# Cross-attention scores in three blocks of four key tiles, and all value products of a batch in one place

## What is computed

```python
q = proj(x1, Wq, bq); k = proj(ctx, Wk, bk); v = proj(ctx, Wv, bv)      # 16 heads of 32
scores = clip(einsum('bhsd,bhtd->bhst', q, k) / sqrt(32), -50, 50)
probs = softmax(where(mask, scores, -50))
out = einsum('bhst,bhtd->bhsd', probs, v) @ Wo.T + bo
x2 = layernorm(x1 + layernorm(clip(rs, 0, 0.3) * out))
```

## Time and profile before

| | |
|---|---|
| median of 3 runs | 1448.34 us (1447.04 to 1449.28) |
| profiled execution, its own time | 1448.77 us |
| its span in the trace | 1446.6 us |
| PE busy | 1415.2 us, 98% |
| DVE busy | 1061.0 us, 73% |
| ACT busy | 681.8 us, 47% |
| POOL busy | 534.1 us, 37% |

### The profile page before, as it was taken

The page is one execution under the profiler, slowest core; times in us unless marked ns, Lnnn a source line. Parts: engine busy times, 40 slices in busy tenths (PEclk is TensorE's granted clock), DMA queues, the critical chain, the costliest instruction groups (busy, mean ns, idle before and its releaser), DMA issues. The chain is left out here.

```text
span 1446.6 us, 31910 instructions
## 1 busy us (share of the span) xinstructions
PE 1415.2 (98%) x13340; PEld 1128.1 (78%) x13340; DVE 1061.0 (73%) x2136; ACT 681.8 (47%) x931; POOL 534.1 (37%) x499
## 2 busy tenths in 40 slices
PE   8999999999999999999999999999999997999998
PEld 4889898987888888888888888888888885555343
DVE  5888676554667777777787768778767777677898
ACT  2444444442434334433343443343343334888996
POOL 1000000000344444445445444444444442753576
PEclk9999999999999999999999999999999999999999
DMA  6526433232221121111211211211211221438895
GB/s 225 164 99 176 131 111 121 94 134 91 99 72 51 45 77 51 52 57 51 79 44 51 72 44 43 79 51 45 71 44 54 69 62 39 108 124 323 279 345 205
DMA packets 93886, 149.41 MB, mean 103 GB/s; under 512 B 14002, under 2 KB 61746, under 8 KB 91954
## 3 DMA queue, kind: packets, MB, share of 16 engines
q1 hardware_dynamic: 93746, 147.41, 31.1%
HBM read 101.25 MB, written 44.04 MB: 100 GB/s over the span
## 5 line engine op out<-in xcount | busy, mean ns | idle before, releaser
L912 POOL TENSOR_TENSOR xa_psum<-xa_pr 125x448 f32<-125x448 f32 x126 | 153.0, 1214 | 300.7 <-DVE xa_pr L1135 300.7
L1135 DVE TENSOR_SCALAR xa_pr<-xa_pr,xa_keep 125x448 f32<-125x448 f32 x384 | 152.2, 453 | 131.5 <-ACT xa_pr L964 131.5
L964 ACT ACTIVATE xa_pr<-xa_bSC 125x1344 f32<-125x1344 f32 x128 | 165.6, 1294 | 120.8 <-PE xa_bSC L1259 120.7
L939 ACT ACTIVATE xa_kf<-xa_bKV,xa_bk 128x376 f32<-128x376 f32 x128 | 73.7, 576 | 192.0 <-PE xa_bKV L1178 192.0
L945 ACT COPY xa_v<-xa_bKV 125x512 f32<-125x512 f32 x96 | 56.3, 586 | 206.8 <-PE xa_bKV L1189 201.1
L1178 PE MATMUL xa_bKV<-left_xn,wA 128*128 128x376 f32 x768 | 149.8, 343 | 0.0
L915 POOL TENSOR_TENSOR xa_psum<-xa_psum,xa_pr 125x448 f32<-125x448 f32 x126 | 146.1, 1159 | 9.9
L1178 PE MATMUL xa_bKV<-xa_cx,wA 128*128 128x376 f32 x768 | 149.3, 343 | 0.0
L1189 PE MATMUL xa_bKV<-wZ,left_xn 128*125 128x512 f32 x576 | 142.0, 395 | 2.1 <-POOL xa_ones L881 1.9
L1189 PE MATMUL xa_bKV<-wZ,xa_cx 128*125 128x512 f32 x576 | 141.1, 393 | 0.0
L1178 PEld LDWEIGHTS xa_bKV<-left_xn,wA 128*128 128x128 f32 x768 | 130.0, 188 | 8.9 <-issue 5.3
(11 more groups left out here) (256 smaller groups left out, 2440.2 us busy)
## 6 DMA issues: line engine op xcount, KB each, us to landing
wraw<-in_ctxT SPq DMA_DIRECT2D x32, 752.0 KB, 4.8
ff_hr<-h_scratch SPq DMA_DIRECT2D x28, 512.0 KB, 6.5
wraw<-in_w SPq DMA_DIRECT2D x7, 1024.0 KB, 5.3
xa_qf<-q_scratch SPq DMA_DIRECT2D x32, 224.0 KB, 4.8
xa_x<-x_scratch SPq DMA_DIRECT2D x28, 256.0 KB, 4.9
x_scratch<-xa_x SPq DMA_DIRECT2D x28, 256.0 KB, 2.0
h_scratch<-ff_hq SPq DMA_DIRECT2D x8, 896.0 KB, 5.1
h_scratch<-ff_hs SPq DMA_DIRECT2D x8, 896.0 KB, 5.3
```

The source lines that it names most:

```text
L912: nc.gpsimd.tensor_tensor(psum01[:], third(h, 0), third(h, 1), ALU.add).then_inc(p01_ok, 1)
L964: nc.scalar.activation(pr[h][:], bSC[0:TW, :, 0:TC * S], ACT.Exp, scale=XSCALE).then_inc(exp_ok, 1)
L1135: nc.vector.tensor_scalar(third(h, t), third(h, t), EM50, bound, ALU.max, ALU.min).then_inc(pr_ok, 1)
```

## The change

It does five things at once.

1. The 12 (head group, key tile) pairs of a batch are scored in three blocks of four tiles, in place of four blocks of three. `score_pieces` says which tiles of which group a block holds. The exponential of a block is two ACT instructions, since a block spans two groups.
2. `attend` of all four groups and then `sums` of both pairs of groups stand in one place, behind the first score block of the next batch. Two groups share a bank: values in the columns 0 to 223, sums in 224 to 447.
3. `psum` is one tile of two groups' width in place of two tiles of one group; one `sums` handles a pair with products 224 wide.
4. DVE's `attended` handles a pair: reciprocal and product are 224 wide. Both stand at the start of the next batch's body. `tail2` and `tail3` both stand at the end of the body.
5. POOL's `norm2` moves from ahead of group 3's sums to the end of the body. PE does keys 0, values 0, keys 1, values 1 of the next batch in a row behind the last score block.

The core of the diff:

```diff
-        psum01, psum = n.sb("psum01", [TW, NJ, S]), [n.sb(f"psum{i}", [TW, NJ, S]) for i in range(2)]
+        psum01, psum = n.sb("psum01", [TW, NJ, S]), n.sb("psum", [TW, NJ, 2 * S])
...
+        score_pieces = (((0, 0, 3, 0), (1, 0, 1, 3)), ((1, 1, 2, 0), (2, 0, 2, 2)), ((2, 2, 1, 0), (3, 0, 3, 1)))
...
# POOL
                 for h in range(C):
-                    if h == 3 and tail is not None and not last(b):
-                        norm2(tail)
                     if not (last(b) and h >= 2):
...
-                        wait(pool, sum_done, 4 * b + h - 1)
-                        nc.gpsimd.tensor_tensor(psum[h % 2][:], psum01[:], third(h, 2), ALU.add).then_inc(ps_ok, 1)
+                        if h % 2 == 0:
+                            wait(pool, sum_done, 2 * b + h // 2)
+                        nc.gpsimd.tensor_tensor(psum[:, :, value_columns(h)], psum01[:], third(h, 2), ALU.add).then_inc(ps_ok, 1)
...
+                if tail is not None and not last(b):
+                    norm2(tail)
# DVE
             def body(b, par, pair):
+                if not first(b):
+                    attended(b - 1, 0)
+                    attended(b - 1, 1)
+                limits(b, 0)
+                if not last(b):
+                    split_low(b + 1, 1 - par)
+                limits(b, 1)
...
+                if tail is not None:
+                    tail1(tail)
+                limits(b, 2)
...
+                if tail is not None and not last(b):
+                    tail2(tail)
+                    tail3(tail)
# PE
+            def sums(b, p):
+                pe.wait_ge(ps_ok, 4 * b + 2 * p + 2)
                 for j in range(NJ):
+                    mm = nc.tensor.matmul(bPV[p][j * HD:(j + 1) * HD, 2 * S:4 * S], ones[0:TW, :], psum[:, j, :], start=True, stop=True)
                 mm.then_inc(sum_done, 1)
...
+            def attend_pairs(b, par, pairs):
+                for p in pairs:
+                    attend(b, par, 2 * p)
+                    attend(b, par, 2 * p + 1)
+                for p in pairs:
+                    sums(b, p)
...
+                scores(b, par, 0)
+                if third_value(b):
+                    keys(b, par, 2)
+                if not first(b):
+                    attend_pairs(b - 1, 1 - par, range(2))
+                if third_value(b) == 0:
+                    keys(b, par, 2)
+                    values(b, par, 2)
+                scores(b, par, 1)
+                keys(b, par, 3)
+                if third_value(b):
+                    values(b, par, 2)
+                if tile_of(b - 1) is not None:
+                    output(b - 1)
+                scores(b, par, 2)
...
+                    for t in range(2):
+                        keys(b + 1, 1 - par, t)
+                        values(b + 1, 1 - par, t)
```

More of the change, by code:

```diff
@@ L827, in third_value, with pair_bank, value_columns, sum_columns @@
             return 1 if b % 8 == 1 else 0
+        score_pieces = (((0, 0, 3, 0), (1, 0, 1, 3)), ((1, 1, 2, 0), (2, 0, 2, 2)), ((2, 2, 1, 0), (3, 0, 3, 1)))
+        def pair_bank(b, h):
+            return bPV[0] if last(b) and h == 3 else bPV[h // 2]
+        def value_columns(h):
+            return slice(h % 2 * S, (h % 2 + 1) * S)
+        def sum_columns(h):
+            return slice((2 + h % 2) * S, (3 + h % 2) * S)
         def third(h, t):
@@ L863, in body @@
                 if not last(b):
[L864 removed]
+                    wait(sp, sc_done, 3 * b)
                     queries(b + 1, 1 - par)
@@ new lines, in low_part @@
+            def low_part(b, h):
+                dve.wait_ge(cthi_ok, 4 * b + h + 1)
+                for lo, size, to in pieces(b):
+                    low = nc.vector.scalar_tensor_tensor(out=cT[1][:, h, to:to + size], in0=at[:, h % 2 * S + lo:h % 2 * S + lo + size],
+                                                         scalar=bvt[:, h:h + 1], in1=cT[0][:, h, to:to + size].bitcast(F32),
+                                                         op0=ALU.add, op1=ALU.subtract)
+                low.then_inc(ctlo_ok, 1)
@@ new lines, in attended @@
+            def attended(b, p):
+                q, bank = 2 * b + p, bPV[p]
+                if first(b) and p == 0:
+                    dve.wait_ge(q_out, 16 * (NG + 1))
+                dve.wait_ge(sum_done, q + 1)
+                nc.vector.reciprocal(rinv, bank[:, 2 * S:4 * S]).then_inc(ri_ok, 1)
+                dve.wait_ge(ri_ok, q + 1)
+                nc.vector.tensor_tensor(at, bank[:, 0:2 * S], rinv, ALU.mult).then_inc(at_ok, 1)
+                if p == 0:
+                    wait(dve, o_done, ((b + 1) * S - 1) // P - CR + 1)
+                dve.wait_ge(at_ok, q + 1)
+                for h in (2 * p, 2 * p + 1):
+                    if not last(b):
+                        high_part(b, h)
+                for h in (2 * p, 2 * p + 1):
+                    low_part(b, h)
@@ new lines, in body @@
+                if not first(b):
+                    attended(b - 1, 0)
+                    attended(b - 1, 1)
+                limits(b, 0)
+                if not last(b):
+                    split_low(b + 1, 1 - par)
+                limits(b, 1)
+                if first(b):
+                    output_weights(0)
+                    output_weights(1)
+                if tail is not None:
+                    tail1(tail)
+                limits(b, 2)
+                if first(b):
+                    output_weights(2)
+                    output_weights(3)
@@ L1175, in keys @@
                 wait(pe, k_ok, 4 * b + m)
+                if m == 0:
+                    wait(pe, clo_ok, b)
                 for c in range(C):
@@ L1230, in attend @@
                                               pr[h][:, j, t * S:(t + 1) * S], start=t == 0, stop=t == TC - 1)
                 mm.then_inc(pv_done, 1)
-            def sums(b, h):
-                s = 4 * b + h
-                bank = bPV[h % 2]
-                if last(b) and h >= 2:
-                    for t in range(TC):
-                        for j in range(NJ):
-                            mm = nc.tensor.matmul(bank[j * HD:(j + 1) * HD, S:2 * S], ones[0:TW, :], pr[h][:, j, t * S:(t + 1) * S],
-                                                  start=t == 0, stop=t == TC - 1)
-                    mm.then_inc(sum_done, 1)
-                    return
-                pe.wait_ge(ps_ok, s + 1)
+            def sums(b, p):
+                pe.wait_ge(ps_ok, 4 * b + 2 * p + 2)
@@ new lines, in sums_one, with scores @@
+            def sums_one(h):
+                for t in range(TC):
+                    for j in range(NJ):
+                        mm = nc.tensor.matmul(pair_bank(B - 1, h)[j * HD:(j + 1) * HD, sum_columns(h)], ones[0:TW, :], pr[h][:, j, t * S:(t + 1) * S],
+                                              start=t == 0, stop=t == TC - 1)
+                mm.then_inc(sum_done, 1)
+            def scores(b, par, block):
+                if block == 0:
+                    pe.wait_ge(q_in[par], 8 * (b - par) + 16)
+                pe.wait_ge(k_ok, 4 * b + block + 2)
+                wait(pe, exp_ok, 6 * b + 2 * block)
+                for i in range(TC + 1):
+                    h, t = divmod((TC + 1) * block + i, TC)
+                    for j in range(NJ):
+                        own = slice(j * HD, (j + 1) * HD)
+                        mm = nc.tensor.matmul(bSC[0:TW, j, i * S:(i + 1) * S], kf[own, h, t * TW:(t + 1) * TW], qf[par][own, h, :],
+                                              start=True, stop=True)
+                mm.then_inc(sc_done, 1)
```

191 lines of the change are left out of this document (67 added, 124 removed).

## The result

The changed kernel takes 1641.0 us (median of 4 runs, 1639.5 to 1643.2), the kernel before 1447.8 us beside it: a ratio of 1.1335, 95% interval 1.132 to 1.135. It is slower by 193 us. The forecast was 1624 us, 17 us too low.

What follows compares the result with a forecast made beforehand. PE, working without pause, was taken to bound the kernel. Longer periods (30.4 us with the gap, 32.0 or 33.1 through DVE) added 168 us and the clock 8 to 1448.8: 1624.8, median 0.4 lower, so 1624 us; range 1575 to 1690.

Steps and rivals of the forecast that it cites:

- The gap: Between a batch's two sums PE waits for three POOL steps, since `psum` is one tile: 3.95 us per batch.
- The forecast's 0.43 us for 512 columns: Price of one fp32 product in PE's sums, making 224 wide sums no dearer than twice as many 112 wide.
- PE's own blocks: PE's work per batch gets shorter by 0.5 us, from 26.95 to 26.45; over 31 batches 15 us.
- the rival "faster": POOL's steps have a free place to write, or PE has other work between sums: 1434 us without gap; chance 0.03.
- DVE's loop: From first sum through POOL, DVE, context load, ACT and PE back: 32.0 us a round, 33.1 where columns wrap.
- the list from the first sum to keys 1: POOL's steps, `norm2`, `tail3`, attended values, clamps, `split_low`, load, ACT's keys copy: 23.0 us until PE can do keys 1.
- The clock: After gaps of 4 us PE may run at half clock a few us: 4 or 5 x 1.7 = 8 us.
- DVE's hold: DVE's `tail3` waits for `norm2`, which stands behind POOL's steps in the gap, and holds the queue behind it.
- the held periods: Batches where DVE waits for `norm2`; the wait at keys 1 swallows the 1.7 us of half clock there.
- The rival that the clock falls after every gap: Low clock lasts into PE's keys 1 to value products: 50 us more, 1675 us; chance 0.13.
- What would show it: Signs listed: PE share near 86%, second sums 4.3 us after first, next reciprocal about 6 us after first sum's end.
- The second wait: PE waits again at keys 1 for ACT's copy of keys, 1 to 2 us, in most batches.

Runs made afterwards that it cites:

- the kernel with the gap alone: Changed kernel plus 20 unread matmuls on PE between the two sums, and DVE's `split_low` moved between `tail2` and `tail3`: 1561.6 us.
- the best one: Changed kernel with two psum tiles, `norm2` ahead of group 2's second step, `x1_beta` at the head of POOL's body, `split_low` ahead of the reciprocals: 1434.4 us.
- 1564: Changed kernel with both `norm2` ahead of POOL's second step of group 2 and 20 unread matmuls on PE between the two sums: 1563.7 us.
- the filler: Changed kernel plus 20 unread matmuls on PE between the sums of the two pairs: 1635.1 us.
- `norm2` early: Changed kernel with POOL's `norm2` moved ahead of the second step of head group 2: 1616.2 us.

## Why the prediction was right, and where it was off

- **The gap: right.** Forecast: second sums 4.3 us after the first, 122 us of waits. Measured: 4.39, and 119.2 us in 31 places. The difference between the kernel with the gap alone (1561.6) and the best one (1434.4) is 127 us, 31 x 4.1. (The forecast's 0.43 us for 512 columns is one of the two instructions of an fp32 product. Its rounds are counted in instructions too, so the sum isn't touched.)
- **PE's own blocks: right, the total in part by luck.** Forecast 26.45 us per period and 1434 us without the gap. In the best version the period is 26.42 us, score blocks are 1.07 apart, and the time is 1434.4. From the batch at 388.00 to the last one it saves 18.7 us (to 1169.25, before to 1187.97), more than the 15 of the forecast, and the end of the cross-attention, for which the forecast has no term, gives 3.6 back. It needed four edits, though; the rival "faster" said only that POOL's steps find a free place to write, and with that alone the kernel took 1472. The 26.42 us are what PE could do, not what the change without its tile would have given.
- **DVE's loop: right in cause and length, wrong in where it closes.** The step that failed is the list from the first sum to keys 1: it stopped DVE's part at `split_low` and went on by the load. `tail3`, a pair at 3.0 us and the issue of the load are as forecast, with two instructions off: `split_low` was not slowed by POOL, and POOL was slowed by it (2.93 in place of 1.16), so SP's issue came 14.5 us behind the first sum's end, not 15 to 16. The queue behind `split_low` was missing: four clamps and the read of the output tile, for which PE waits at its values block. I had priced clamps at 1.17 / 3, from a place where POOL ran only `norm2` on one column (545.13). By luck the longer branch was about as long: forecast 32.0 and 33.1, measured 32.2 and 33.2.
- **The clock: about right in the sum, far more of it than thought.** I gave it 8 us, 1.7 us in each of four or five batches where DVE isn't held. Every gap was followed by the half clock, up to 74 us of PE's work in all. Alone it costs 52 us (1616 against 1564); on top of DVE's hold it costs 6 (1641 against 1635), or 14 by the estimate above. The forecast's sentence that the wait in the held periods swallows it, and in the others doesn't, was right: in the four batches with b % 8 = 2 the changed kernel takes 1.3 to 2.3 us more than the filler's, 6 together, and in the held ones it is swallowed in all but four. The rival that the clock falls after every gap had half of its condition met: it fell after every gap, but was up again at most 6.4 us behind the gap's end, well ahead of keys 1. Its price, 50 us on top of the loop, was not paid, since the loss lay where DVE would have been waited for. By the Trainium skill (TensorE: Matmul & The Clock Gate, "Loop structure matters more than you think") a long wait ahead of a matmul sends the array back to its lower clock, each time round the loop. The trace agrees for gaps of 3.8 us, 31 times of 31.
- **The 17 us that are missing.** The mis-sized terms are the periods, by 7 us, and the end, by 10. From the first score block at 388.00 to that of the last batch the changed kernel takes 983.5 us and the kernel before 800.0, so 183.5 more, where the forecast with its clock term has 176. From the last batch's first score block to the last output product the kernel before takes 28.2 us, the changed one 38.2, the best one 31.8. DVE's hold was sized about right: 61 us in the sum, 63 by the estimate above. The forecast has no term for the end: there the two pairs of batch 30 and the last batch's own first pair all stand behind one another, with a wait of 2.50 us for `cT` and the half clock (timeline of PE in the changed kernel):

```profile
1396.49 0.78 PE L1264 MATMUL xa_bPV<-xa_pr,xa_v 125*32 125x112 f32 x24 [1.20 <-DVE xa_pr L1156]
...
1401.39 2.93 PE L1242 MATMUL xa_bKV<-wQ,xa_cT 128*128 128x512 f32 x6 [2.50 <-DVE xa_cT L1036]
```
- **What would show it.** PE's share was 90%, not 86: half-clock work counts as busy. The next reciprocal began 5.5 us after the first sum's end, forecast 6. The second wait was looked for at the keys and was, hardly visible, at the values.

Open: what sets the moment at which the clock falls around a gap. How long it stays low goes with that moment: in the changed kernel and with `norm2` early, all stretches of 6.8 us at a gap began 0.5 to 1.9 us ahead of the second sums, all of 3.4 us from 0.4 us ahead of them to 1.4 behind. Open too is what decides whether clamps alternate with POOL's instructions or run through. I didn't try the change's score blocks without its move of the value products.

## What to carry to other kernels

When a change brings two consumers of one buffer together, look at the buffer's count before the order of anything else: here one tile cost 169 us of 193, and its second copy fitted by filling it in place and laying the mask into it. A waiting engine costs what is behind it in its queue up to the last instruction that somebody else waits for, not only up to the first. When two costs are suspected, switch off each and both: alone they seemed worth 25 and 6 us and together were worth 77, and either single experiment would have told the wrong story. Look also at what the edit that switches a cost off leaves of it: the filler left 38 of 167 us at half clock.
